# Flamingo block on one core: maxima 1.75 units ahead, weights' maxima over two batches, and the seams of the FFN block

## The reference, cut to what matters

```python
x = x + tanh(g_xattn) * xattn(layernorm(x), ctx, ctx, Wq, bq, Wk, bk, Wv, bv, Wo, bo)
x = x + tanh(g_ffn) * ffn(layernorm(x), ...)
# xattn: q, k, v = projections; q, k rotated (rope)
#        softmax(q k^T / 4) v, then Wo and bo
# ffn:   s_x = sigmoid(clip_x) * max|x| / 127            (one maximum over the whole tensor)
#        xq  = clip(round(x / s_x), -128, 127) * s_x
#        h   = silu(xq Wg^T) * (xq Wu^T)                 (Wg, Wu, Wd rounded per row to 127 * s_row)
#        h   = the same rounding with one maximum over all of h; out = h Wd^T
```

## Time and profile before

| what | value |
|---|---|
| median of three runs | 604.42 us (602.25 to 606.8) |
| the profiled execution: its time, its span | 602.7 us, 600.9 us |
| PE busy, DVE busy, ACT busy, POOL busy | 565.9, 533.6, 442.1, 253.7 us |
| first block, second block, third block begin at | 0, 107.7, 509.0 us |

### The profile page before, as it was taken

One profiled execution on the slowest core, in us unless ns is written; L12 is line 12 of the kernel. 1 busy time (PEld: TensorE's weight loads), 2 busy tenths in 40 slices (PEclk: granted clock), 3 DMA queues, 4 the chain that ended last, 5 costly groups with the idle time before them and its releaser, 6 DMA issues. The chain is left out here.

```text
span 600.9 us, 18561 instructions
## 1 busy us (share of the span) xinstructions
PE 565.9 (94%) x6592; PEld 262.3 (44%) x6592; DVE 533.6 (89%) x693; ACT 442.1 (74%) x873; POOL 253.7 (42%) x371
## 2 busy tenths in 40 slices
PE   7999999998899989999999999999999989888985
PEld 3655655233344434444444444444444433333364
DVE  4799989999999979899899899899899775799888
ACT  2667667257777877797797797798798672788694
POOL 8599989701333434214214215215214311665400
PEclk8999999999999999999999999999999999999999
DMA  8759887542332334233333234235222000000035
GB/s 290 242 161 302 244 189 214 139 104 69 73 76 60 73 65 73 53 84 76 53 75 84 53 69 89 53 64 86 62 62 48 3 2 0 2 2 0 0 106 176
DMA packets 61255, 55.21 MB, mean 92 GB/s; under 512 B 11040, under 2 KB 58784, under 8 KB 61216
## 3 DMA queue, kind: packets, MB, share of 16 engines
q1 hardware_dynamic: 61216, 54.70, 36.2%
HBM read 37.62 MB, written 16.78 MB: 91 GB/s over the span
## 5 line engine op out<-in xcount | busy, mean ns | idle before, releaser
L908 ACT ACTIVATE prob<-st_ps 128x512 f32<-128x512 f32 x512 | 280.7, 597 | 71.3 <-PE st_ps L765 64.2
L765 PE MATMUL st_ps<-q,k 98*32 98x512 bf16 x2048 | 178.9, 380 | 6.1 <-ACT prob L908 4.9
L968 DVE TENSOR_REDUCE negm<-xT_ps 128x2 f32<-128x1024 f32 x128 | 154.6, 1207 | 8.4 <-PE xT_ps L338 7.8
L968 DVE TENSOR_REDUCE negm<-v_ps 128x2 f32<-128x1024 f32 x128 | 154.4, 1206 | 6.3 <-PE v_ps L338 6.3
L789 PE MATMUL pv_ps<-prob,v_u 128*32 128x512 f32 x1024 | 132.8, 592 | 0.7 <-ACT prob L908 0.7
L765 PEld LDWEIGHTS st_ps<-q,k 98*32 98x32 bf16 x2048 | 56.9, 95 | 96.3 <-ACT prob L908 41.1
L338 PE MATMUL xT_ps<-k,q 96*32 96x512 bf16 x1024 | 78.4, 379 | 1.4 <-DVE negm L968 1.3
L338 PE MATMUL v_ps<-k,q 96*32 96x512 bf16 x1024 | 78.4, 380 | 1.1 <-DVE negm L968 1.0
L1157 POOL TENSOR_TENSOR msplit<-negm,onesf 128x16 bf16<-128x16 f32 x32 | 7.1, 223 | 129.8 <-DVE negm L968 129.8
L1177 POOL TENSOR_TENSOR normal<-turned,recip 128x256 f32<-128x256 f32 x32 | 19.9, 622 | 78.7 <-DVE recip L982 78.7
L789 PEld LDWEIGHTS pv_ps<-prob,v_u 128*32 128x32 f32 x1024 | 31.8, 110 | 25.8 <-issue 2.0
(11 more groups left out here) (153 smaller groups left out, 807.6 us busy)
## 6 DMA issues: line engine op xcount, KB each, us to landing
qk_parts<-parts SPq DMA_DIRECT2D x96, 128.0 KB, 2.7
k<-qk_parts SPq DMA_DIRECT2D x192, 64.0 KB, 2.7
q<-qk_parts SPq DMA_DIRECT2D x192, 64.0 KB, 3.0
ctx<-in_ctxT SPq DMA_DIRECT2D x8, 512.0 KB, 4.7
X<-in_x SPq DMA_DIRECT2D x8, 512.0 KB, 8.5
out<-X SPq DMA_DIRECT2D x7, 512.0 KB, 2.9
q<-mrow SPq DMA_DIRECT2D x64, 4.0 KB, 2.6
wf<-in_w_down SPq DMA_DIRECT2D x1, 704.0 KB, 5.0
```

What stands on the lines that cost most here:

```text
L765: last = nc.tensor.matmul(score_bank(i)[lo:lo + COLS, :], k6[g][:, h, kt * P + lo:kt * P + lo + COLS], q6[g][:, h, :], start=True, stop=True)
L908: nc.scalar.activation(prob[kt % 2][:, h, :], score_bank(HPU * kt + h)[:], ACT.Exp, scale=SCALE).then_inc(exp_done, 1)
L968: nc.vector.tensor_reduce(negm[g % 2][:, lo:lo + 2], pair[:], op=ALU.max, axis=AX.X, negate=True).then_inc(mx_read, 1)
```

## The change

1. The two filler matmuls at the end of the first block go.
2. `TURN_SLOT` is 8: the maxima are turned after key tile 1, not 0, and the bank order follows. In unit u DVE and PE do in key tile 0 the last head of unit u + 1, and in key tiles 1 to 3 heads 0 to 2 of unit u + 2 (`ahead_unit`). The prologue has two calls less, unit 2 of batch 7 has two more. The wait for a unit's loads moves to key tile 1.
3. SP sends the mrow rows of unit 0 ahead of the last store of batch 7, and the loads of unit 3 ahead of the wait for all stores; this wait is for batches 0 and 1 first, for all after batch 0.
4. The weights' largest values: six jobs of two rows, two of 704, two tiny; one in every third key tile of batches 0 and 1. POOL's `prepare_weights` is in batch 2, behind `x1_means`; only woT stays in batch 1.
5. In batch 7 the weight transposes and what follows them move one key tile on.
6. FFN: ACT scales chunk 1 of x, not POOL. In the last pair the last three slots are reduced as one slot ahead of DVE's last product and two slots behind it, where it was two slots and one, both behind. DVE scales group 1 of h itself; the first output is scaled after the first clip of chunk 1, not after the second.

```diff
@@ first block, PE
-                stay_busy(k_ps[:, 1, :], END_A)
@@ second block
-        TURN_SLOT = HPU
+        TURN_SLOT = 2 * HPU
+        def ahead_unit(b, g, kt):
+            g2 = g + (2 if kt else 1)
+            return (b, g2) if g2 < UPB else (b + 1, g2 - UPB)
+        def is_ahead(b, g, kt):
+            return not is_last(b) or g < 2 or (g == 2 and kt == 0)
+        WJOBS = NIC + KC + 2
@@ SP
                 load_unit(sp, 0, 2)
-                for i in range(4):
+                for i in range(3):
                     store(sp, B - 1, i)
                 max_rows(0, 0)
+                store(sp, B - 1, 3)
+                load_unit(sp, 0, 3)
+                for i in range(4):
+                    sp.wait_ge(stored[i], 2 * NSTORE)
+                body(0)
                 for i in range(4):
                     sp.wait_ge(stored[i], B * NSTORE)
-                over_batches(sp, body, B, True)
+                with sp.Fori(1, B - 1) as b:
+                    body(b)
+                body(B - 1)
@@ PE
-                    query_scores(mg, kt, j, pair_bank(g, kt, j))
+                    query_scores(mg, (kt + 3) % 4, j, pair_bank(g, kt, j))
...
-                        pe.wait_ge(exp_done, 16 * u + 2)
+                        pe.wait_ge(exp_done, 16 * u + TURN_SLOT - 2)
...
+                            ahead = is_ahead(b, g, kt)
+                            if ahead and kt == 1:
+                                mb, mg = ahead_unit(b, g, kt)
+                                pe.wait_ge(unit_in[mg], NLOAD * (mb + 1))
...
-                            if is_last(b) and g >= 2 and 4 * (g - 2) + kt < NWT:
-                                weight_transpose(4 * (g - 2) + kt)
-                            if is_last(b) and g == 3 and kt == 1:
+                            if is_last(b) and 0 < 4 * (g - 2) + kt <= NWT:
+                                weight_transpose(4 * (g - 2) + kt - 1)
+                            if is_last(b) and g == 3 and kt == 2:
                                 down_scales()
...
-                            if kt == 0 and not (is_last(b) and g == 3):
+                            if kt == 1 and not (is_last(b) and g == 3):
                                 max_transpose(b, g)
...
-                            if g or h:
+                            if (g or h) and not (g and h == HPU - 1):
@@ DVE
-                                maxima(mb, mg, kt, 0, pair_bank(g, kt, 0))
+                                maxima(mb, mg, (kt + 3) % 4, 0, pair_bank(g, kt, 0))
...
-                            if is_first(b):
-                                weight_maxima(TPB * g + kt)
+                            if isinstance(b, int) and b < 2:
+                                n, wait = divmod(16 * b + TPB * g + kt, 3)
+                                if not wait and n < WJOBS:
+                                    weight_maxima(n)
...
-                    if n < 12:
-                        nc.vector.tensor_reduce(wmax[:, n:n + 1], wf[:, n, :], ...)
+                    if n < NIC:
+                        rows = slice(2 * n, 2 * n + 2)
+                        nc.vector.tensor_reduce(wmax[:, rows], wf[:, rows, :], ...)
@@ POOL
-                        if isinstance(b, int) and b == 1:
-                            prepare_weights(g)
+                        if isinstance(b, int) and b == 1 and g == 0:
+                            nc.gpsimd.tensor_tensor(woT[:], wo_raw[:], ...)
...
                             x1_means(pool, b - 1)
+                        if isinstance(b, int) and b == 2:
+                            prepare_weights(g)
@@ third block, ACT
+                nc.scalar.activation(xi[1], V[:, 4:8, :], ACT.Copy, scale=ainv[:, 0:1]).then_inc(xs_ready, 1)
...
                 for m in range(PAIRS * NG):
-                    scale_h(m)
+                    if m != 1:
+                        scale_h(m)
@@ DVE
+                        if s == SLOTS - 1 and last_pair(p):
+                            largest_of(0, SLOTS - 3, SLOTS - 2)
...
+                        if s == SLOTS - 1 and last_pair(p):
+                            largest_of(1, SLOTS - 2, SLOTS)
...
-                for j in (4, 5):
-                    largest(PAIRS - 1, j)
...
+                dve.wait_ge(ascale_ready, 2)
+                nc.vector.tensor_scalar(hi[1], hst[:, 2:4, :], ainv[:, 1:2], None, ALU.mult).then_inc(hs_first, 1)
...
-                        if n and j == 1:
+                        if n and j == (n > 1):
                             scale_out(n - 1, 0, 4)
@@ POOL
-                pool.wait_ge(ascale_ready, 1)
-                nc.gpsimd.tensor_scalar(xi[1], V[:, 4:8, :], ainv[:, 0:1], None, ALU.mult).then_inc(xs_ready, 1)
```

More of the change, by code:

```diff
@@ L711, in wait_score_bank @@
             else:
-                back = next(j for j in range(16) if slot(j) == slot(i) - 3) if slot(i) != TURN_SLOT + 3 else 1
+                back = next(j for j in range(16) if slot(j) == slot(i) - 3) if slot(i) != TURN_SLOT + 3 else TURN_SLOT - 3
                 eng.wait_ge(exp_done, n + back + 1)
+        def ahead_unit(b, g, kt):
[3 more added lines that the diff above has]
+            return not is_last(b) or g < 2 or (g == 2 and kt == 0)
         def pair_bank(g, kt, j):
@@ L743, in body @@
                         nb, ng = (b + 1, g - 1) if g else (b, 3)
-                        if not (is_last(b) and g):
-                            if not (is_first(b) and g == 0):
-                                sp.wait_ge(st_ready, 16 * u)
+                        if not (is_last(b) and g) and not (is_first(b) and g == 0):
+                            sp.wait_ge(st_ready, 16 * u)
                             load_unit(sp, nb, ng)
@@ L853, in body @@
                         u = UPB * b + g
-                        mb, mg = (b, g + 2) if g < 2 else (b + 1, g - 2)
-                        ahead = not (is_last(b) and g >= 2)
-                        if ahead:
-                            pe.wait_ge(unit_in[mg], NLOAD * (mb + 1))
                         pe.wait_ge(mrow_in[g], MROWS * DMA * (b + 1))
                         for kt in range(TPB):
+                            ahead = is_ahead(b, g, kt)
+                            if ahead and kt == 1:
+                                mb, mg = ahead_unit(b, g, kt)
+                                pe.wait_ge(unit_in[mg], NLOAD * (mb + 1))
                             for h in range(HPU):
@@ L1043, in body @@
                             if ahead:
-                                maxima(mb, mg, kt, 1, pair_bank(g, kt, 1))
+                                maxima(mb, mg, (kt + 3) % 4, 1, pair_bank(g, kt, 1))
                             if kt == 3 and g == 0 and not is_first(b):
@@ L1048, in body @@
                                 turn_back(b, 0)
-                            if is_last(b) and g >= 2 and TPB * (g - 2) + kt < B - 2:
-                                x1_largest(TPB * (g - 2) + kt)
+                            if is_last(b) and 0 < TPB * (g - 2) + kt <= B - 2:
+                                x1_largest(TPB * (g - 2) + kt - 1)
                             if is_last(b):
@@ L1075, in weight_maxima @@
                         dve.wait_ge(late_in, 11 * DMA)
[L1076 to L1079 removed]
+                    if n < NIC:
+                        rows = slice(2 * n, 2 * n + 2)
+                        nc.vector.tensor_reduce(wmax[:, rows], wf[:, rows, :], op=ALU.max, axis=AX.X, apply_absolute_value=True).then_inc(w_step, 1)
+                    elif n < NIC + KC:
+                        i = n - NIC
                         nc.vector.tensor_reduce(wmax[:, WD + i:WD + i + 1], wd[:, i, 0:INNER], op=ALU.max, axis=AX.X,
                                                 apply_absolute_value=True).then_inc(w_step, 1)
[L1082 to L1083 removed]
+                    elif n == NIC + KC:
+                        dve.wait_ge(w_step, NIC + KC)
                         for lo, hi in ((0, 2 * NIC), (WD, NROW)):
@@ L1107, in _ @@
                         maxima(0, 0, h, j, mx_ps[j])
-                for h in range(HPU):
+                for h in range(HPU - 1):
                     for j in range(2):
@@ L1240, in _ @@
                 body(1)
-                with pool.Fori(2, B - 1) as b:
+                body(2)
+                with pool.Fori(3, B - 1) as b:
                     body(b)
@@ L1313, in build @@
         hs_ready = sem("hs_ready")
+        hs_first = sem("hs_first")
         hq_ready = sem("hq_ready")
@@ L1524, in _, with largest_of @@
                 LARGEST = {1: (1, 4), 2: (1, 5), 3: (0, 0), 5: (0, 1), 7: (0, 2), 9: (0, 3)}
+                def largest_of(col, lo, hi_):
+                    for s in range(lo, hi_):
+                        wait_product(dve, PAIRS - 1, s)
+                    nc.vector.tensor_reduce(hmax[:, NG * PAIRS - 2 + col:NG * PAIRS - 1 + col], hst[:, SLOTS * (PAIRS - 1) + lo:SLOTS * (PAIRS - 1) + hi_, :],
```

(8 more changed lines are left out.)

28 lines of the change are left out of this document (11 added, 17 removed).

## The result

The changed kernel took 596.83 us as a median of 4 runs (595.78 to 598.83), the kernel before 603.34 in the same comparison (602.04 to 606.8): a ratio of 0.9898, with a 95% interval of 0.9871 to 0.9924. The forecast was 595.6 us. The profiled execution took 595.78 us with a span of 594.0 (before 602.7 and 600.9), so 6.9 us went where the sum said 8.8.

What follows compares the result with a forecast made beforehand. PE was taken to pace batches 3 to 5, DVE batch 0, and several engines in turn the FFN. The terms sum to -8.8 us, giving 593.9 from the profiled 602.7 and 595.6 from the median 604.42; range 592.0 to 600.5.

Steps and rivals of the forecast that it cites:

- end of the first block: First block's end: without PE's filler the block ends with DVE, -0.26 us, no clock effect charged; -0.3 in the sum.
- prologue and batch 0: Attention start: DVE is full, so two fewer maxima reads and lighter weight reductions shorten it; -4.4 us (-6.0 to -2.2).
- batch 1: Attention batch 1: means before casts remove 3.3 us of waiting, late DVE jobs cost +0.7; -2.6 us.
- batches 2 to 6: Later attention batches: transposes one key tile later still arrive in time and PE is full; 0 us (-1 to +1).
- last batch: Last attention batch: two added score calls and later transposes cost at most 1.2 us, at least nothing; +0.4.
- start of FFN (amax to first gate matmul): FFN start: gscale speeds up once POOL's scaling goes to ACT; -0.6 us (-0.9 to +0.3).
- gate and up, with their end: End of gate and up: a short reduction moves ahead of DVE's last product; -0.3 us (-0.6 to +0.2).
- start of down to the last addition: Start of down: DVE takes one ACT scaling and the first output precedes a clip; -1.0 us (-1.3 to -0.4).
- 1 (the stall moves to batch 2): Batch 2: POOL's layer norm ahead of the casts makes a split or the means late; +3.3 us, 598.9, chance 0.20.
- 2: Attention: two-row reductions cost as 256 elements do and PE loses less at each unit; 593.0 us, chance 0.12.
- 3: Batches 0 and 1: waits and late jobs eat DVE's relief, and the seams give nothing; 601.6 us, chance 0.06.
- 4 (row maxima late in every unit): PE's first score of each unit: turned maxima arrive late, 0.5 us in 28 units, +14.0; 609.6 us, chance 0.04.

Runs made afterwards that it cites:

- e12: e10 with six weight casts moved from unit 0 of batch 2 to unit 1, and the clip order of before; 596.37 us, ratio 0.9894.
- e10: The kernel before with all of the change except the maxima's new distance and SP's new order; 597.78 us, ratio 0.9901.
- e6: The changed kernel with the weights' reductions reading 2 elements a row instead of 256 or 704; 594.16 us.
- e11: The changed kernel, unchanged, run again on the same chip as e10 and e12; 597.01 us, ratio 0.9887.
- e3: The kernel before with maxima 1.75 units ahead, turn in key tile 1, and SP's new order of stores, row maxima and loads; 605.8 us.
- e2: The kernel before with maxima 1.75 units ahead, turn in key tile 1 and batch 7's transposes moved on, SP's order as before; 606.31 us.
- e5: The kernel before with two POOL statements swapped, so batch 1's means come ahead of the weights' casts; 599.01 us.
- e4: The kernel before with only the filler at the first block's end removed and the FFN seams changed; 601.59 us.
- e1: The kernel before with only the weights' reductions in every third key tile of batches 0 and 1, casts in batch 2 behind the means; 598.65 us.
- e7: The changed kernel with a 128x1024 POOL scaling put back at the FFN start, into an unread buffer; 596.14 us.
- e8: The changed kernel with the down stage's clips in the order of before; 594.68 us.
- e9: e8 with the ten weight jobs moved to key tiles of batches 1 and 2 without a turn, and casts to batch 3; 596.8 us.

## Why the prediction was right, and where not

By the profiled executions, each forecast term with what the ruler and the stamps gave:

| term | forecast | measured |
|---|---|---|
| end of the first block | -0.3 | -0.31 |
| prologue and batch 0 | -4.4 | -3.56 |
| batch 1 | -2.6 | -2.54 |
| batches 2 to 6 | 0 | 0.0 |
| last batch | +0.4 | +0.90 |
| start of FFN (amax to first gate matmul) | -0.6 | -0.64 |
| gate and up, with their end | -0.3 | -0.07 |
| start of down to the last addition | -1.0 | -0.69 |
| sum | -8.8 | -6.9 |

One mechanism failed, DVE as the bound of batch 0; the others held, and the rest of the miss of 1.9 us is in sizes. Two things flatter the total. The -3.56 includes the 0.80 of the late landing in the kernel before. And the forecast of 595.6 is only 1.2 under the median of 596.83 because it was taken from a median of 604.42, of three runs, which a fourth brought down to 603.34. That is luck, not insight.

*End of the first block* was right: 0.24 by DVE's idle time, the rest of the 0.31 is the moving start., on which the prediction charged nothing for the clock, do not cover this stage, but the granted clock was 1.00 from 100 to 120 us in every trace.

*Prologue and batch 0* was mis-sized by 0.84 in this execution (by 0.03 to 0.84 in the four), and the size that came out hides two errors. The step that failed is "what leaves DVE before batch 0 ends moves that end, as DVE is full". 98% busy was taken for a limit, with one microsecond of the kernel for each of DVE. The weights' part took 2.6 us from DVE there; e12 and e10 won 2.15 against the kernel before, of which 0.80 is that execution's own late landing: 1.35, half. e6 took 3.2 more and won 1.09. What the two calls fewer of the prologue bring with SP's order came out near the forecast of 1.8 (-2.2 and +0.4 of waiting): 1.7 by e11 against e12, 1.4 to 2.2 over the four profiles. But it did so only beside the weights' part; in e3, without it and with a late landing, the same edit lost. The second error is the reading of the earlier trace rows: the 4.5 us from the second issue to PE's start were taken as what this transfer costs behind its loads. Here it was 2.85 (130.86 to 133.71). Where PE waited for them, issues up to 130.9 reached it in 2.9 to 3.0 us, while those of the kernel before and e3, at 131.5, took 4.5 and 4.3. That of e2, at 132.68, was no such case: it landed 1.7 us after its issue. Whether the issue's time or chance made those two late is open. The idle 1.82 us that the prediction read beside the 4.5 is that of the weight load; PE's matmuls stood 0.94.

*Batch 1* was right to 0.1, by its steps too: the order on POOL 3.25 (e5), and against it the forecast 0.7, of which e6 shows that the reductions make most, though not that it is job 6. What it missed is the tail: in e2, e3 and e4 the clock dropped after the same stall, and where it does so in the kernel before, the change removes about 1.4 us more. Whether this is a part of the 6.5 us between the medians is not shown: no run without a profile shows where its clock fell.

*Batch 2* was costed at nothing because the split is wanted later. e1 and e10, without the later turn, lost 1.6 us there; with it, 0.

*Last batch*: items 2 and 5 cost 0.90 us there in every kernel that has them, e2 and e3 included, and nothing in e1, e10 and e12. The two added score calls are the work that is new; how much falls to them and how much to the moved transposes no run parts. The upper bound of 1.2 was nearer than the value taken.

*FFN*: gscale as forecast, and e7 shows the cause that the prediction argued: POOL beside it. As to the rule of the Trainium skill (SBUF — State Buffer, "Who interferes with whom"): the interference is there and the rule's direction decides the term, but not as exclusion for a whole instruction, since in e7 gscale ended at 506.00 and DVE's next clips ran from 505.92 at their usual pace, while POOL worked until 507.72. Whether gscale ran in a two-port mode no run shows. At the *end of gate and up* the short reduction ahead of the last product gains 0.07, next to nothing. At the *start of down* the first output won its 1.02, and 0.33 of it went at the second, through the new clip order (e8), an edit that the prediction mentioned and did not price.

The rivals: 1 (the stall moves to batch 2) did not happen in the changed kernel, but is real without the later turn. 2 did not: the two-row reductions took 0.674 us, not 0.406, and the later batches were not shorter. 3 came true in part: about half of DVE's relief in batch 0 was eaten, by the coupling with PE more than by the waits that it named, and the seams gave what e4 shows. 4 (row maxima late in every unit) did not happen: batches 2 to 6 are unchanged to 0.05 us.

## What to carry to other kernels

When two engines pass work through two banks, an engine that is 98% busy need not be the limit: the worth of a microsecond taken from it was a third to a half here, and a kernel with that work cut short told so. An order of statements on a side engine can be worth more than a deeper look-ahead on the main one: two statements swapped brought 3.2 us, and with one more such move the look-ahead became unnecessary. Parts of a change don't add: try each alone and all but each. Here the look-ahead was a loss alone, in one run with a late transfer; beside the other parts it won 1.7 us in batch 0, gave 0.9 back in the last, and covered another part's stall of 1.6.

## What the runs showed of the hardware

- The granted clock went to half for 6.8 us in e2 after PE's wait of 2.17 us, for 3.4 in e3 after one of 2.37, and for 3.4 in each of e2, e3 and e4 after the wait of 2.7 in batch 1 (PEclk 0.50 and 0.52 in the rows above). In the profiled kernel before, after the same wait of 2.71 us, it did not. The stall in batch 1 was 1.4 to 1.5 us dearer with the fall than without.
- The times of the kernel before tend to go with the mean clock: in the comparison of e9 to e11 four of its runs with a mean clock of 0.996 took 601.91 to 604.28 us (three of them up to 602.41), those with 0.993 took 604.11 to 604.24, those with 0.991 took 604.89 to 605.33. One stretch of 3.4 us at half clock is 0.003 of the mean, by estimate. The mean doesn't say where the clock fell: the profiled kernel before has 0.995, and its half-clock stretches lie from about 12 to 15 us and in the last 2 us, none in the attention. The runs of e10 had 0.997 to 0.999 and lie within 1.6 us of each other; two runs of e11 with 0.997 lie 3.4 apart.
- A 12-column operation of DVE took 1.09 us beside a POOL operation of 3.14 us and 0.23 us without it, while the larger DVE operation ahead of it, 0.49 us, began before POOL's and was not slowed. The two clips behind it, 0.48 us together, ran beside POOL and were not slowed either (0.51 without POOL).
